# A mask matmul over 128 rows instead of 16, five score tiles in the last group, and the last two output turns side by side

## The reference

```python
xn = _layernorm(x)
x = x + attn(xn) + ffn(xn)

def attn(x):                       # 16 heads of 16, causal
    q, k, v = heads(x @ Wq + bq), heads(x @ Wk + bk), heads(x @ Wv + bv)
    q, k = rotary(q), rotary(k)
    att = (einsum('bhid,bhjd->bhij', q, k) + bias[None]) * (1.0 / math.sqrt(D))
    att = softmax(where(causal, att, -inf))
    return einsum('bhij,bhjd->bhid', att, v).reshape(B, T, C) @ Wp + bp

def ffn(x):                        # C = 16 columns of N = 64 neurons
    logits = similarity(x, col_emb) + sigmoid(gelu(x @ gate_w1 + gate_b1) @ gate_w2 + gate_b2)
    mask = one_hot(top_1(logits))
    weights = mask * softmax(logits)
    cols = gelu(einsum('bsd,cdn->bscn', x, W_cols) + b_cols) * weights[..., None]
    y = cols.reshape(Bq, Sq, -1) @ proj_w + proj_b + x
    return layernorm(y) * ln_g + ln_b
```

## Time and profile before

| | us |
|---|---|
| runs, median of 3 | 1976.82 |
| runs, lowest and highest | 1974.98, 1978.83 |
| the profiled execution | 1979.27 |
| its span, first to last instruction | 1977.3 |
| PE busy in the span | 1810.0 (92%) |
| DVE busy | 1548.7 (78%) |
| ACT busy | 1111.8 (56%) |
| POOL busy | 783.6 (40%) |

### The profile page before, as it was taken

How to read it: one execution, slowest core, us unless ns; L and a number is a source line. 1 busy time by engine, 2 the same in 40 slices (tenths; PEclk the granted TensorE clock), 3 DMA queues, 4 the chain that set the end, 5 groups by cost and what they waited for, 6 DMA issues and landing times.

```text
span 1977.3 us, 35087 instructions
## 1 busy us (share of the span) xinstructions
PE 1810.0 (92%) x10870; PEld 1041.7 (53%) x10870; DVE 1548.7 (78%) x5438; ACT 1111.8 (56%) x2150; POOL 783.6 (40%) x1018
## 2 busy tenths in 40 slices
PE   5779999999999999999999999999999999999877
PEld 3555555555556555555555555565555555555433
DVE  4568888878877887888887888787888788777783
ACT  3326555566655566665555666555666555655544
POOL 6553444343444344344434344433434443311110
PEclk9789999999999999999999999999999999999998
DMA  6673233333233323433333332332333232232201
GB/s 185 181 176 92 76 90 97 105 97 102 89 95 100 111 65 97 123 90 88 99 97 90 112 93 75 104 109 79 97 102 106 85 103 85 60 87 72 58 12 49
DMA packets 220469, 189.44 MB, mean 96 GB/s; under 512 B 63387, under 2 KB 195371, under 8 KB 220284
## 3 DMA queue, kind: packets, MB, share of 16 engines
q1 hardware_dynamic: 219840, 186.83, 33.4%
q10 hardware_dynamic: 444, 0.38, 0.1%
HBM read 118.64 MB, written 69.27 MB: 95 GB/s over the span
## 4 chain that ended last, share of the span: by engine, by line
PE 56%; DVE 26%; ACT 8%; issue 6%; DMA 1%; POOL 1%; SPq 1%; DVEq 0%; ACTq 0%; POOLq 0%
PE scores L1273 10%; PE rows L1210 10%; PE o_bank L1189 9%; PE scores L1172 8%; PE bank L1284 7%; DVE scores L1357 5%; DVE rows L1379 5%; DVE maxima L1384 5%; ACT probs L1051 4%; PE bank L1302 3%; PE bank L1234 3%; PE scores L1275 2%; DVE maxima L1379 2%; PE bank L1228 1%; DVE scores L1359 1%
## 5 line engine op out<-in xcount | busy, mean ns | idle before, releaser
L1051 ACT ACTIVATE probs<-scores 128x512 f32<-128x512 f32 (+1 forms) x1280 | 671.6, 555 | 511.6 <-DVE scores L1357 296.6
L1384 DVE TENSOR_REDUCE maxima<-rows 128x1 f32<-128x512 f32 (+4 forms) x896 | 479.9, 552 | 166.8 <-PE rows L1210 163.1
L1172 PE MATMUL scores<-stack_q,stack_k 99*128 99x512 bf16 (+3 forms) x1536 | 430.5, 331 | 79.3 <-ACT probs L1051 70.4
L1210 PE MATMUL rows<-stack_k,stack_q 96*128 96x256 bf16 (+3 forms) x2048 | 459.4, 290 | 15.8 <-DVE maxima L1379 6.8
L1379 DVE CUSTOM_DVE_ANT_0 rows<-rows,near_rows 128x256 f32<-128x256 f32 (+1 forms) x1024 | 394.5, 431 | 54.8 <-PE rows L1210 54.1
L1357 DVE TENSOR_TENSOR scores<-scores,near_cols 128x256 f32<-128x256 f32 x768 | 320.7, 430 | 67.6 <-PE scores L1172 67.4
L1210 PEld LDWEIGHTS rows<-stack_k,stack_q 96*128 96x128 bf16 x2048 | 175.0, 98 | 313.6 <-issue 112.8
L1189 PE MATMUL o_bank<-probs,v_aug 128*32 128x512 f32 (+3 forms) x3072 | 317.5, 501 | 2.8 <-ACT probs L1051 2.8
L1273 PE MATMUL scores<-again,w_cols 128*128 128x256 f32 x1024 | 275.2, 391 | 3.6 <-DMA b_cols<-in_b_cols_dram 3.6
L1172 PEld LDWEIGHTS scores<-stack_q,stack_k 99*128 99x128 bf16 x1536 | 139.9, 97 | 254.8 <-ACT probs L1051 195.7
L1284 PE MATMUL bank<-w_proj,act_t 128*128 128x256 f32 x1024 | 255.4, 382 | 14.6 <-DVE y L1414 14.2
(11 more groups left out here) (123 smaller groups left out, 2138.8 us busy)
## 6 DMA issues: line engine op xcount, KB each, us to landing
parts_d<-part SPq DMA_DIRECT2D x96, 256.0 KB, 2.2
stack_q<-parts_d SPq DMA_DIRECT2D x378, 64.0 KB, 3.1
stack_k<-parts_d SPq DMA_DIRECT2D x378, 64.0 KB, 2.3
kept_d<-kept SPq DMA_DIRECT2D x31, 512.0 KB, 2.9
again<-kept_d SPq DMA_DIRECT2D x31, 512.0 KB, 3.5
x<-in_x_dram SPq DMA_DIRECT2D x32, 256.0 KB, 3.4
turns<-turns_d SPq DMA_DIRECT2D x32, 256.0 KB, 3.0
v_d<-v SPq DMA_DIRECT2D x32, 256.0 KB, 2.4
```

Of the source, the lines that this page charges most:

```text
L1051: act.activation(probs[:, (g * NS + s) % PROBS, h, 0:width], ring[(rings + ring_n[1]) % RING][:, 0:width], ACT.Exp, scale=float(D) ** -0.5 ...
L1172: ins = pe.matmul(ring[(rings + ring_n[1]) % RING][:, c0:c0 + w], stack_k[g % 2][:, h, kb * P:(kb + 1) * P], stack_q[g % 2][:, h, q0:q0 + ...
L1210: ins = pe.matmul(tile[:, c0:c0 + k1 - k0], stack_q[ag % 2][0:STACK, h, qb * P:(qb + 1) * P], stack_k[ag % 2][0:STACK, h, k0:k1], start=Tr ...
L1384: ins = dve.tensor_reduce(maxima[:, part, m:m + n], tile[:, c0:c0 + n * w].rearrange("p (n w) -> p n w", w=w), AX.X, ALU.max)
```

## The change

It has three parts.

1. The mask matmul works over 128 rows. `pick` becomes a tile of 128 rows, filled with zeros by GpSimd, and ACT's cast writes its first 16 rows after that fill. `others` gets 128 columns for each block of tokens, zero beyond the 16 that DVE writes. The two transposes of `mask_turn` have 128 output rows instead of 16, ACT copies all of them, and `others_t` has 128 rows. All added products are zero times zero. `FILLS` goes from 5 to 7.
2. In the last group of the last batch the two `row_ring` banks take score tiles too. `score_tile` deals the tiles out over five banks: the two row banks, then the three ring banks. PE's wait becomes the exponential of the tile five before.
3. For the last batch's chunks 2 and 3, both `y_turn` stages come ahead of both projections; chunk 3's turned output goes to `ffn_t` (the second half of `again`), which no neurons use any more. SP loads `result` for chunk 3 in the stage `y_turn` of chunk 3 instead of after chunk 2's store.

```diff
@@ -276,6 +276,7 @@
             o.add("y_turn", NG - 1, k)
+        for k in range(NC // 2, NC):
             o.add("project_begun", NG - 1, k)
@@ -375,7 +376,7 @@
         turns = sb("turns", [P, 2, 2, CH])
-        pick = sb("pick", [E, EM * P], BF16)
+        pick = sb("pick", [P, EM * P], BF16)
         near_rows = sb("near_rows", [P, H, 2 * P])
@@ -411,12 +412,12 @@
         first = sb("first", [P, CT])
-        others = sb("others", [P, CT, E])
+        others = sb("others", [P, CT, P])
         below = sb("below", [P, CT, E])
...
         weight = sb("weight", [P, NC, CT])
-        others_t = sb("others_t", [E, NC, CH], BF16)
+        others_t = sb("others_t", [P, NC, CH], BF16)
         act_t = sb("act_t", [P, EM, CH])
@@ -540,6 +541,22 @@
+        def closing_group(b, g):
+            return b == B - 1 and g == NG - 1
+        def score_tile(b, g, arg, at):
+            if not closing_group(b, g):
+                return ring[at % RING]
+            slot = arg[0] * GH + arg[1]
+            place = slot % (RING + 2)
+            return row_ring[place] if place < 2 else ring[(at - slot + place - 2) % RING]
+        def turned(b, g, arg):
+            return ffn_t if closing_group(b, g) and arg == NC - 1 else y_t
         def projected(b, g):
@@ -819,6 +836,11 @@
                                 .then_inc(rest_in_done[k], 16)
+                    elif stage == "y_turn" and arg == NC - 1 and closing_group(b, g):
+                        sp.wait_ge(result_out[1], b * (NC // 2 * 16) + 2 * 16)
+                        alone(sp)
+                        sp.dma_start(result[:, 1], rest_d[b, :, arg * CT:(arg + 1) * CT, :]).then_inc(rest_in_done[1], 16)
                     elif stage == "project":
@@ -826,7 +848,7 @@
                         k = arg + 1
-                        if 2 <= k < NC:
+                        if 2 <= k < (NC - 1 if closing_group(b, g) else NC):
@@ -847,6 +869,7 @@
             fills += [(stack_k[i][STACK:STACK + 3], 1.0) for i in range(2)]
+            fills += [(pick[:, :], 0.0), (others[:, :, :], 0.0)]
             assert len(fills) == FILLS
@@ -1023,7 +1046,8 @@
             act.activation(ident_b[:, :], ident[:, :], ACT.Copy).then_inc(cast, 1)
-            act.activation(pick[:, :], act_t[0:E, 1:5, :].rearrange("p m n -> p (m n)"), ACT.Copy) \
+            act.wait_ge(filled, FILLS)
+            act.activation(pick[0:E, :], act_t[0:E, 1:5, :].rearrange("p m n -> p (m n)"), ACT.Copy) \
                 .then_inc(cast, 1)
@@ -1049,7 +1073,7 @@
                         act.activation(probs[:, (g * NS + s) % PROBS, h, 0:width],
-                                       ring[(rings + ring_n[1]) % RING][:, 0:width], ACT.Exp,
+                                       score_tile(b, g, arg, rings + ring_n[1])[:, 0:width], ACT.Exp,
                                        scale=float(D) ** -0.5).then_inc(ring_drained, 1)
@@ -1092,7 +1116,7 @@
                         act.wait_ge(bank_filled[i], use + 1)
-                        act.activation(others_t[:, c, :], bank[0:E, 0:CH], ACT.Copy).then_inc(bank_drained[i], 1)
+                        act.activation(others_t[:, c, :], bank[:, 0:CH], ACT.Copy).then_inc(bank_drained[i], 1)
                     elif stage == "shift_turn":
@@ -1111,7 +1135,7 @@
                         for t in range(CT):
-                            ins = act.activation(y_t[:, :, t * P:(t + 1) * P],
+                            ins = act.activation(turned(b, g, arg)[:, :, t * P:(t + 1) * P],
                                                  bank[:, t * C:(t + 1) * C].rearrange("p (k n) -> p k n", n=P),
@@ -1163,13 +1187,18 @@
                         s, h = arg
-                        pe.wait_ge(ring_drained, tile_n + 1)
+                        if not closing_group(b, g):
+                            pe.wait_ge(ring_drained, tile_n + 1)
+                        elif s * GH + h < 2:
+                            pe.wait_ge(rows_drained, B * NG * len(ALL_ROWS) + 2)
+                        else:
+                            pe.wait_ge(ring_drained, tile_n - 1)
                         if s == 0 and h == 0:
...
                             w = (half + 1) * HALF - q0
-                            ins = pe.matmul(ring[(rings + ring_n[1]) % RING][:, c0:c0 + w],
+                            ins = pe.matmul(score_tile(b, g, arg, rings + ring_n[1])[:, c0:c0 + w],
                                             stack_k[g % 2][:, h, kb * P:(kb + 1) * P],
@@ -1250,7 +1279,7 @@
                         for t in range(CT):
-                            ins = pe.transpose(bank[0:E, t * P:(t + 1) * P], others[:, t, :], ident[:, :])
+                            ins = pe.transpose(bank[:, t * P:(t + 1) * P], others[:, t, :], ident[:, :])
                         ins.then_inc(bank_filled[i], 1)
@@ -1299,7 +1328,7 @@
                             for k in range(KC):
-                                ins = pe.matmul(bank[:, t * C:(t + 1) * C], y_t[:, k, t * P:(t + 1) * P],
+                                ins = pe.matmul(bank[:, t * C:(t + 1) * C], turned(b, g, arg)[:, k, t * P:(t + 1) * P],
                                                 w_out[:, k, :], start=(k == 0), stop=(k == KC - 1))
@@ -1351,7 +1380,7 @@
                         near = near_cols[:, g * GH + h, :]
-                        tile = ring[(rings + ring_n[1]) % RING]
+                        tile = score_tile(b, g, arg, rings + ring_n[1])
                         ins = (dve.tensor_tensor(tile[:, 0:P], tile[:, 0:P], near[:, P:2 * P], ALU.add)
@@ -1492,7 +1521,7 @@
                         step(6)
-                        dve.tensor_tensor(others[:, :, :], ranked[:, :, :], each(first[:, :]), ALU.not_equal) \
+                        dve.tensor_tensor(others[:, :, 0:E], ranked[:, :, :], each(first[:, :]), ALU.not_equal) \
                             .then_inc(chosen, 1)
@@ -1544,7 +1573,7 @@
 NEAR_LOADS = 3 * P // SHEARED
-FILLS = 5
+FILLS = 7
 PADS = 4
...

```

## The result

Four runs of the changed kernel took 1928.21 to 1931.58 us, median **1930.09 us**; four of the kernel before, 1974.98 to 1978.83, median 1977.22. The ratio is 0.9762, 95% interval 0.9745 to 0.9779: faster by 2.4%. The forecast was 1936.7, its range 1926 to 1956.

What follows compares the result with a forecast made beforehand. The prediction took TensorE (busy 92%) as the bound up to each group's last row tile, VectorE's steps behind it. 29.6 + 1.5 + 2.6 + 2.8 + 1.6 + 2.0 = 40.1 us off 1976.82 gave 1936.7, range 1926 to 1956.

Steps and rivals of the forecast that it cites:

- The five masks: Masks up to each group's last row tile, where TensorE is the bound: 0.98 us a group, 29.6 us in 30 groups.
- The three masks behind: Masks after the last row tile, beside VectorE's steps: nothing in half the groups, 0.1 us in 15 others, 1.5 us.
- the 36 of the forecast: Sign: TensorE's summed wait for o_turn's output at the columns matmul should grow from 14.2 to 36 us.
- The transfers of the shift: TensorE's waits for transfers bringing the shift into stack_q, outside the last group, should go: 2.6 us in 7 waits.
- The prologue: Its 16 masks in two groups: 2.0 us in the second, 0.8 taken for the first, together 2.8 us.
- Part 2 (forecast 1.6, bounds 0 and 2.3): Five score tiles in the last group: two thirds of 2.3 us of waits for exponentials should go.
- Part 3 (forecast 2.0, up to 1.7 more): Last turns: second projection directly follows the first, 2.0 us; up to 1.7 more if the clock returned before it.
- The forecast's check: Sign at the kernel's end: the two last projections should run as sixteen pieces without a gap.
- The clock rival: Longer columns waits lower the clock: one to six groups, 1940 to 1956, chance 0.07; most groups, 2036, chance 0.04.
- the forecast's 3.3 us a fall: Upper cost of one clock fall: half of 6.57 us busy in a 6.9 us low-clock stretch near 1841.
- the reason given against the rival: Twelve microseconds of unbroken TensorE work stand before the columns wait, and nearly three behind it.
- its 32.6: Forecast gain for 29 main-loop groups: 29 of the 30 times 0.98, plus 1.5 and 2.6 us.

Runs made afterwards that it cites:

- 64-row kernel: Changed kernel with the mask matmul reading only the first 64 of its 128 rows: 1971.84 us, ratio 0.9964 to the kernel before.
- work added ahead of and behind the last row tile: Two runs of the changed kernel with mask matmuls repeated: first five pieces once more, 1945.80 us; last three pieces twice more, 1937.30 us.
- three kernels with gaps: The kernel before (1977.22 us), the changed kernel with part 1 taken back (1971.78 us), and that with 64 mask rows (1971.84 us).
- Part 1 alone: Kernel before with only the 128-row mask matmul, its two fills and the wait for them: 1934.43 us, ratio 0.9776.
- 96-row kernel: Changed kernel with the mask matmul reading only 96 of its 128 rows: 1928.78 us, ratio 0.9746 to the kernel before.
- kernel of parts 2 and 3 alone: Changed kernel with part 1 taken back (16 mask rows, five fills): 1971.78 us, ratio 0.9960 to the kernel before.
- the output's copy early: Changed kernel with VectorE's third output copied right behind the shift: 1933.20 us, ratio 0.9782 to the kernel before.
- one step more: Changed kernel with the output copied early and each column piece waiting only for the neurons tile it reads: 1931.06 us, ratio 0.9753 to the kernel before.
- the other 0.27: Changed kernel with the output copied early and the shift's transpose ahead of the last neurons piece: 1919.66 us, ratio 0.9703 to the kernel before.
- both together: Changed kernel with the output copied early, columns waiting by pieces, and the shift's transpose early: 1912.54 us, ratio 0.9671 to the kernel before.

## Why the prediction was right, and where its sizes were not

**The cause and the bound.** The argument was that a matmul over 16 rows costs TensorE 0.10 us on the way in and 0.10 out, 0.20 out before float32, that depth cures it, and that five of eight are on the path. All three steps held: 0.86 and 0.11 us as forecast, the 64-row kernel brings the loss back, and work added ahead of and behind the last row tile shows the split.

**The five masks (forecast 29.6).** The stretch from the first mask to the last row tile lost 0.91 us a group, and the gap ahead of the first mask, which lies outside that stretch, 0.10: 30 x 1.01 = 30.4 us. Right.

**The three masks behind (forecast 1.5).** Measured 30 x 0.19 = 5.6 us. This is the term that failed in its working. There are three kinds of groups, and I had read two. In the first kind (14 groups, is one) the gain is 0, as forecast. In the second (12 groups, is one) it is 0.19 us, not 0.1: VectorE's step ahead of the output and the output itself stood 0.29 us apart, start to start, and in the changed kernel this is 0.11, since consecutive steps overlap:

```profile
1278.74 0.19 DVE L1516 TENSOR_TENSOR ranked<-tied,rank 128x32 f32<-128x32 f32 x1
1278.85 0.25 DVE L1440 RECIPROCAL inv<-bank 128x16 f32<-128x16 f32 x1
```

The third kind are the last four groups with neurons. They have no statistics and no choice for a later chunk, so VectorE is through early and waits for TensorE's transposes, and all three masks count: 0.85 us in each, 3.4 us. Timeline of such a group in the trace of before, and of after:

```profile
1820.63 0.61 PE L1210 MATMUL rows<-stack_k,stack_q 96*128 96x512 bf16 x3
...
1826.25 2.86 PE L1284 MATMUL bank<-w_proj,act_t 128*128 128x256 f32 x12 [0.37 <-DVE y L1414]
```

```profile
1776.95 0.60 PE L1239 MATMUL rows<-stack_k,stack_q 96*128 96x512 bf16 x3
...
1780.94 0.26 DVE L1440 RECIPROCAL inv<-bank 128x16 f32<-128x16 f32 x1 [0.89 <-PE bank L1320]
...
1781.72 0.48 PE L1313 MATMUL bank<-w_proj,act_t 128*128 128x256 f32 x1 [0.37 <-DVE y L1443]
```

5.62 us became 4.77, and the wait at the columns matmul stayed 0.37. That is also why this wait is 33.8 us in all and not the 36 of the forecast: in four groups it did not grow.

**The transfers of the shift (forecast 2.6).** Measured 0.8 in the list of waits: those besides the last group's fell from 2.6 us in 7 to 1.8 in 6. The list leaves out what is under 0.15 us; by the starts, from the columns matmul to the first score, it is 1.5 us, the one fall of the clock below left out. I had read that the transfers' issue moves ahead by 0.8 us more than the score that waits. In the groups that waited before, the wait shrank by 0.02 to 0.33 us and in two by all of it, and two new groups wait 0.20 and 0.34: how long the transfers take varies by as much, which a single margin from one group doesn't cover.

**The prologue (forecast 2.8).** Measured 8.8 in the traces shown. Take the masks at the forecast's 2.8 us. 1.1 us lie ahead of the first mask of all (86.7 us before, 85.6 after), where the twelve traces spread from 85.5 to 88.0 with gaps or without. The rest goes with the clock, by the records and not by an experiment: in the trace of before it is at its lower level, 1.2 GHz, for 10.2 us up to 141.0, with the second group's neurons stage begun, and in the changed kernel for 6.8 us up to 132.5. Window sums of before and of after, and the stretch of each that holds both prologue groups:

```profile
130.80:141.00 10.20, 7.62 (x20) 4.09 (x21) 6.95 (x23) 1.47 (x3) 7.49 (x10) 0.50 0.82 215
```

```profile
125.70:132.50 6.80, 4.49 (x13) 2.64 (x14) 6.17 (x21) 0.63 (x1) 6.39 (x9) 0.50 0.66 180
```

```profile
76.00:196.00 120.00, 99.39 (x507) 59.59 (x511) 84.86 (x290) 47.44 (x93) 48.88 (x62) 0.90 0.57 146
```

```profile
76.00:196.00 120.00, 97.76 (x554) 63.66 (x552) 90.84 (x311) 51.50 (x102) 46.99 (x63) 0.94 0.58 151
```

A granted clock of 0.94 instead of 0.90 over 120 us is 4.8 us of full clock, which with 2.8 and 1.1 makes 8.7. The forecast read the earlier trace rows, a stretch with a granted clock of 0.78, and had no term for the clock in it; that is the step. It repeats: in the three kernels with gaps the main loop's first mask starts at 192.4 to 195.2 us, in the other nine, those with added masks among them, at 185.0 to 187.9. But the length of that low stretch is not a clean mark of the gaps (6.8 us in seven of the nine and 10.2 in two, against 10.2 to 13.7), and why they shorten it no run here shows.

**Part 2 (forecast 1.6, bounds 0 and 2.3).** 31.63 - 29.40 = 2.2 us, just under the upper bound, and in four kernels of the kind 2.6 or 2.7, above it. No score in the last group waits for an exponential any more; I had let a third come back, and none did.

**Part 3 (forecast 2.0, up to 1.7 more).** 16.4 - 13.9 = 2.5 us here, 1.9 to 2.8 in five of the others, and 5.0 in the four whose clock did not fall there, where the forecast's two numbers reach 3.7. The forecast's check fails in a detail. Timeline of the end:

```profile
1914.77 1.94 PE L1325 MATMUL bank<-ident,y 128*128 128x128 f32 x8 [0.90 <-DVE y L1443]
1915.89 0.66 ACT L1138 ACTIVATE y_t<-bank 128x256 f32<-128x256 f32 x2 [2.80 <-PE bank L1325]
1916.74 0.66 ACT L1138 ACTIVATE again<-bank 128x256 f32<-128x256 f32 x2 [0.20 <-PE bank L1325]
1917.55 3.72 PE L1331 MATMUL bank<-w_out,y_t 128*128 128x256 f32 x8 [0.84 <-ACT again L1138]
1921.10 1.90 PE L1331 MATMUL bank<-w_out,again 128*128 128x256 f32 x8
```

The sixteen pieces do run without a gap, and the second eight at full clock, from 1921.1. But the first projection starts 2.8 us behind the first turn, because it waits for the second copy; before, with one turn and one copy ahead, it was 1.5 us (1963.16 to 1964.63). What the first loses the second more than gains. I had not named this price of two turns ahead. It comes from the program and not from the data: chunk 2's projection reads `y_t` and writes the bank that the first copy emptied, but its wait is looked up as that of the latest `y_turn`, which is now chunk 3's. The first copy ends at 1916.55 and the second at 1917.40, so a wait for its own turn's copy should end some 0.85 us earlier, an estimate; that was not tried.

**The clock rival.** It happened once. Timeline of TensorE, and window sums:

```profile
763.42 4.54 PE L1313 MATMUL bank<-w_proj,act_t 128*128 128x256 f32 x12 [1.76 <-DVE y L1443]
```

```profile
764.00:767.40 3.40, 3.40 (x10) 2.68 (x9) 0.77 (x5) 0.00 (x0) 3.40 (x4) 0.50 0.01 2
```

After the longest of the 30 waits, 1.76 us, the clock is at 1.2 GHz for 3.4 us (the forecast's 3.3 us a fall came from a stretch of 6.9), and from the columns matmul to the first score it takes 4.38 us instead of 2.69: 1.7 us lost. Part 1 alone and the 96-row kernel show it at the same place. But the kernel with more work ahead of the last row tile has the same 1.76 us wait there, and its columns and scores then follow at full clock:

```profile
769.76 2.86 PE L1316 MATMUL bank<-w_proj,act_t 128*128 128x256 f32 x12 [1.76 <-DVE y L1446]
```

So the length of the wait alone does not decide it. The other 29 waits, up to 1.4 us, left the clock alone, which fits the reason given against the rival but does not isolate it.

**In sum** the main loop gained 4.5 us more than its 32.6. By the starts in its 29 groups, 26.7 us lie between the first mask and the last row tile, 4.8 from there to the columns matmul, -0.2 from there to the first score (1.5 of the transfers, less the 1.7 of the fall), and 5.8 from the first score to the next first mask. Of these 5.8, the gap ahead of the first mask is 2.9, and 2.7 lie in two groups alone, whose periods fell from 56.38 to 53.09 us and from 53.58 to 50.49. Those are the two late groups with a low stretch of the clock, 6.8 us of it in each before and 3.4 after. One of before is in the earlier trace rows; window sums of one of after:

```profile
1692.40:1695.80 3.40, 3.40 (x15) 1.11 (x16) 1.96 (x9) 1.96 (x4) 0.94 (x2) 0.50 0.52 170
```

The masks are not what shortened them: in the kernel of parts 2 and 3 alone, which keeps all gaps, the same two periods are 54.83 and 52.22 us, 1.6 and 1.4 less than before, again with 3.4 us of low clock each. So these 2.7 us go with the clock and not with the masks, and the forecast had no term for them. Why the low stretches are shorter no run here shows.

From the last neurons stage to the end the terms add up to 6.3 us (0.7, 0.85, 2.2 and 2.5) where 5.0 were gained. From that stage's first score to the end of the last group's wait for the shift it takes 1.1 us longer than before, with 9.8 us at the lower clock instead of 3.1. The prologue gave 6 us more than its term. Of the 10.8 us by which the traces beat the forecast's sum, 3.8 are in the profiled pair and not in the medians. In the traces the masks gave 4.9 us more than forecast, and the clock 5.8 on balance (4.8 and 2.7, less the 1.7), for which the forecast had no term.

## What to carry to other kernels

A small matmul amid full ones is priced by its neighbours' starts, not by its own duration: 273 against 280 ns said nothing, 0.96 against 0.86 and 0.21 against 0.11 said all, and so does a weight load that starts together with its own matmul. Padding it with zeros beyond 64 rows took 2.2% off this kernel for two fills. To find what a saving is worth, find the instruction of the stage at which another engine's row of steps begins, and count only what stands ahead of it; but do so for each kind of group, the last ones and the prologue too. And where two chains end within half a microsecond of each other, a step on one of them gives little until the other is shortened too: with the output's copy early, one step more took 0.04 us off the stretch from the last row tile to the first score, the other 0.27, and both together 0.87 (2, 14 and 21 us of the medians, which come from two chips; 6, 16 and 22 by the ratios).

## What the runs showed of the hardware

- The gap around a matmul of few rows is the same at 16 and at 64 rows and absent at 96 and 128: 0.10 us going in, 0.10 coming out before bfloat16 of 96 rows and 0.20 before float32. It goes with a weight load that starts only with its own matmul. The matmul rows count it as busy time; the rows of the weight loads show it as idle.
- GpSimd's fill of 128 partitions with 1024 bfloat16 each took 1.92 us, where 3 partitions with 4096 each took 3.51: more than twice as long per element of a partition, and I had estimated 0.9. The 256 float32 took 0.34, under 0.5 as estimated. GpSimd's wait behind shrank from 6.09 to 5.04 us, so it cost nothing:

```profile
8.41 1.92 POOL L877 MEMSET pick<- 128x1024 bf16 x1
...
17.95 0.24 POOL L904 TENSOR_SCALAR norm<-moments 128x2 f32<-128x2 f32 x1 [5.04 <-DVE moments L1459]
```

- The same step seems to stand ahead of the multiplication with v, whose weights are 32 columns wide: there too the first weight load starts within 2 ns of its own matmul, in all 317 places of the changed kernel's trace where no idle time of TensorE stands ahead of it. Timeline of TensorE in the changed kernel:

```profile
1210.73 0.38 PE L1239 MATMUL rows<-stack_k,stack_q 96*128 96x256 bf16 x2
1211.04 0.86 PE L1218 MATMUL o_bank<-probs,v_aug 128*32 128x256 f32 x16
```

Two matmuls of 256 columns take 0.22 us to the next one elsewhere, and 0.31 here. It was not tried; if it is the same thing, it stands ahead of every such block of this kernel.
